# Memory stage of a decoder kernel: gated values formed on GpSimd in token layout

## The reference

```
sim = einsum('pbnhd,hkpd->bn..', q, keys)              # 8 heads, 2 sides, 32 keys
s, i = top_k(sim, 8) on both sides; scores = top 8 of the 64 sums
o = einsum('bnd,bnhkd->bnhk', inputs, key_in[idx])     # inputs . down vector
o = gelu(o, approximate=False) * softmax(scores)
return einsum('bnhk,bnhkd->bnd', o, key_out[idx])
```

## Time and profile before

| what | value |
|---|---|
| median of three runs | 2621.1 us |
| profiled execution, its own time | 2621.93 us |
| its span, first to last instruction | 2620.1 us |
| mean granted TensorE clock | 0.951 of full speed |
| PE busy | 2343.8 us (89%) |
| PEld busy | 1855.1 us (71%) |
| DVE busy | 2078.6 us (79%) |
| ACT busy | 1887.8 us (72%) |
| POOL busy | 836.3 us (32%) |
| memory stage, L1243's first start to the end of L1846's last | 583.7 us to 1309 us |

### The profile page before, as it was taken

The page is one execution under the profiler, slowest core; times in us unless marked ns, Lnnn a source line. Parts: engine busy times, 40 slices in busy tenths (PEclk is TensorE's granted clock), DMA queues, the critical chain, the costliest instruction groups (busy, mean ns, idle before and its releaser), DMA issues.

```text
span 2620.1 us, 95472 instructions
## 1 busy us (share of the span) xinstructions
PE 2343.8 (89%) x34892; PEld 1855.1 (71%) x34892; DVE 2078.6 (79%) x5455; ACT 1887.8 (72%) x3592; POOL 836.3 (32%) x1203
## 2 busy tenths in 40 slices
PE   2999943966999999999889999899899999999999
PEld 1676632645888888888857667566688788888887
DVE  6788889668899999999667777688766777777776
ACT  1888852777688888878467777788567777777776
POOL 1455510336566666666333333233100000000000
PEclk9999975987899999999899999899799999999999
DMA  5000000000000000000020000111011111111111
GB/s 183 1 0 0 0 17 1 1 0 3 2 0 0 0 0 0 0 0 0 3 66 0 0 0 0 36 43 44 30 43 46 49 56 52 57 51 54 52 57 45
DMA packets 56808, 64.82 MB, mean 25 GB/s; under 512 B 7696, under 2 KB 35088, under 8 KB 56592
## 3 DMA queue, kind: packets, MB, share of 16 engines
q1 hardware_dynamic: 56720, 63.65, 7.9%
HBM read 59.17 MB, written 4.46 MB: 24 GB/s over the span
## 4 chain that ended last, share of the span: by engine, by line
PE 68%; DVE 17%; issue 9%; ACT 2%; SPq 1%; DVEq 1%; POOL 1%; ACTq 0%; POOLq 0%; DMA 0%
PE ps L1075 5%; PE ps L1118 5%; PE ps L1103 5%; PE ps L1348 4%; PE ps L1370 4%; PE ps L1372 4%; PE ps L1371 4%; PE ps L1350 4%; PE ps L1349 4%; PE ps L1131 3%; PE ps L1090 3%; DVE work L1829 2%; PE ps L1248 2%; DVE work L1830 2%; DVE work L1836 2%
## 5 line engine op out<-in xcount | busy, mean ns | idle before, releaser
L559 POOL TENSOR_TENSOR work<-work,consts_sb 128x1024 f32<-128x1024 f32 x128 | 245.9, 1921 | 387.8 <-ACT work L727 346.9
L1260 PE MATMUL ps<-work 32*32 32x32 f32 x16384 | 249.5, 224 | 45.7 <-DVE work L1779 31.6
L1260 PEld LDWEIGHTS ps<-work 32*32 32x32 f32 x16384 | 242.2, 145 | 60.3 <-issue 60.3
L1988 DVE TENSOR_TENSOR h_low<-consts_sb,h_up 128x1024 fp32r<-128x1024 f32 x128 | 156.7, 1224 | 116.1 <-ACT h_up L964 116.1
L1586 DVE TENSOR_REDUCE work<-ps 128x8 f32<-128x512 f32 x256 | 169.8, 686 | 86.0 <-PE ps L1075 80.1
L1348 PE MATMUL ps<-a_low,w_up 128*128 128x512 f32 x512 | 205.9, 402 | 0.0
L1370 PE MATMUL ps<-h_low,d_up 128*128 128x512 f32 x512 | 199.9, 390 | 2.3 <-DVE h_low L1988 2.3
L1350 PE MATMUL ps<-a_up,w_low 128*128 128x512 f32 x512 | 200.7, 392 | 0.0
L1349 PE MATMUL ps<-a_up,w_up 128*128 128x512 f32 x512 | 200.6, 392 | 0.0
L1372 PE MATMUL ps<-h_up,d_low 128*128 128x512 f32 x512 | 199.5, 390 | 0.0
L1371 PE MATMUL ps<-h_up,d_up 128*128 128x512 f32 x512 | 199.2, 389 | 0.0
(11 more groups left out here) (297 smaller groups left out, 6271.5 us busy)
## 6 DMA issues: line engine op xcount, KB each, us to landing
gates_spread<-gate_rows SPq DMA_DIRECT2D x128, 256.0 KB, 3.1
ctxT_all<-in_ctxT SPq DMA_DIRECT2D x1, 4096.0 KB, 12.9
work<-in_ctx SPq DMA_DIRECT2D x64, 64.0 KB, 1.7
work<-in_ctxT SPq DMA_DIRECT2D x64, 64.0 KB, 1.7
out<-x_all SPq DMA_DIRECT2D x16, 256.0 KB, 3.5
big<-in_up SPq DMA_DIRECT2D x1, 2048.0 KB, 8.5
consts_sb<-in_consts SPq DMA_DIRECT2D x1, 936.0 KB
w<-in_key_inT SPq DMA_DIRECT2D x1, 512.0 KB, 3.3
```

Source lines behind the costliest of these rows:

```text
L559: pool.tensor_tensor(KX[:, u].rearrange("p b (h k) -> p b h k", h=PER_SET), KC[:, u].unsqueeze(2).to_broadcast([P, 2, PER_SET, SEQ]), own_ ...
L1260: ins = pe.matmul(psW[rows, n // 16, :, n % 16], XT[rows, T.u, :, n], YT[rows, T.u, :, n], start=True, stop=True)
L1988: dve.tensor_tensor(h_low[:, n], hid[n], h_up[:, n].bitcast(F32), ALU.subtract).then_inc(h_split, 1)
```

## The change

The gating moves from the expert layout to the token layout. `hidden` on TensorE now has the tile's tokens as the stationary operand (two matmuls of 512 columns), so gelu's output lies with tokens on partitions. Because the stationary operand is taken from a fixed buffer, SyncE copies each tile of xT into XH (a transfer from SBUF to SBUF) two tiles ahead. GpSimd's new segment `gated` multiplies WT with HT in place, TensorE's `turn_gated` transposes the product into psG, and ScalarE's new segment `copy_gated` copies psG to HG. VectorE's `gated` is gone. The lags behind it grow by one: `turn_gated` 6, `mixed` 7, `add_memory` 6, the statistics 8. IN2 becomes two buffers, and `terms` waits for `scaled_one_hots` of two tiles earlier.

```diff
--- before.py
+++ after.py
@@ -250,15 +250,16 @@
         Z = carve(2 * PH).rearrange("p (u h) -> p u h", u=2)
         FLOOR = carve(2 * PH).rearrange("p (u h) -> p u h", u=2)
         RZ = carve(2 * PH).rearrange("p (u h) -> p u h", u=2)
-        hots = carve(3 * 2 * NS).rearrange("p (r s h k) -> p s r h k", r=3, s=2, h=PH)
-        IN2 = hots[:, :, 2]
+        hots = carve(4 * 2 * NS).rearrange("p (r s h k) -> p s r h k", r=4, s=2, h=PH)
+        IN2 = [hots[:, :, 2 + u] for u in range(2)]
         KI = carve(NEXP)
         sides = carve(8 * NS)
         XY = sides.rearrange("p (k n h) -> p n h k", n=8, h=PH)
         XT = carve(2 * NEXP).rearrange("p (u k t) -> p u k t", u=2, k=NKEY)
         YT = carve(2 * NEXP).rearrange("p (u k t) -> p u k t", u=2, k=NKEY)
         WT = carve(NEXP)
-        HT = carve(2 * NEXP).rearrange("p (u c d) -> p u c d", u=2, c=CHUNKS)
+        HT = carve(2 * NEXP).rearrange("p (u n) -> p u n", u=2)
+        XH = carve(2 * P).rearrange("p (u d) -> p u d", u=2)
         HG = w8[:, 0:NEXP].rearrange("p (c d) -> p c d", c=CHUNKS)
 
 
@@ -285,7 +286,7 @@
         x_side, y_side = [sides.rearrange("p (k a n) -> p k a n", k=NKEY, a=4)[:, :, a:4:2] for a in range(2)]
 
         def one_hots_of(u):
-            return hots[:, :, u:3:2 - u]
+            return hots[:, :, u:4:2]
 
         HC = HID // P
         QUAD = 4
@@ -363,7 +364,7 @@
         psW = ps[:, 0:2, :].rearrange("p q (k t) -> p q k t", k=NKEY)
         psABOVE = ps[:, 2:4, :].rearrange("p q (n h k) -> p (q n) h k", n=2, h=PH)
         psG = ps[:, 4:6, :].rearrange("p b (c d) -> p (b c) d", d=P)
-        psH = ps[:, 6:8, :].rearrange("p b (c d) -> p (b c) d", d=P)
+        psH = ps[:, 6:8, :]
         psM = bank(4, 0)
         psSim = ps[:, 0, :]
 
@@ -430,8 +431,9 @@
         scaled_ready, best_less_ready = sem("scaled_one_hots_ready"), sem("best_less_ready")
         share_ready, xy_ready, sides_ready, spread_done, back_ready, back_turned = (
             sem("share_ready"), sem("xy_ready"), sem("sides_ready"), sem("spread_done"), sem("back_ready"), sem("back_turned"))
-        h_done, h_ready, hg_ready, m_done = sem("h_done"), sem("h_ready"), sem("hg_ready"), sem("m_done")
+        h_done, h_ready, gated_ready, hg_ready, m_done = sem("h_done"), sem("h_ready"), sem("gated_ready"), sem("hg_ready"), sem("m_done")
         y_used_x, y_used_m = sem("xout_used"), sem("memory_used")
+        raw_in = [sem("raw_tile0_in"), sem("raw_tile1_in")]
 
         lg_done, lg_ready, lg_less_max, le_ready = sem("lg_done"), sem("lg_ready"), sem("lg_less_max"), sem("le_ready")
         a_step, a_split, w_step, w_split = sem("a_step"), sem("a_split"), sem("w_step"), sem("w_split")
@@ -484,6 +486,12 @@
                 sp.dma_start(kout[NKEY * j:NKEY * j + NKEY], key_out.rearrange("(a c j) d -> j a c d", a=NKEY, c=CHUNKS)[j])\
                     .then_inc(tables, 16)
 
+            sp.wait_ge(phase, PHASE["memory"])
+
+            def raw_tile(T):
+                need(sp, h_done, T.before(2))
+                sp.dma_start(XH[:, T.u, :], xTt[:, T.t, :]).then_inc(raw_in[T.u], 16)
+            staggered(nc, sp, NT, [(0, raw_tile)])
             sp.wait_ge(phase, PHASE["attn1"])
             sp.dma_start(up_w, up.rearrange("e p h -> p e h")).then_inc(experts_in, 16)
             sp.dma_start(down_w, down.rearrange("e (c p) d -> p e c d", p=P)).then_inc(experts_in, 16)
@@ -623,16 +631,15 @@
                 x, y = keys_of(u)[:, 0], keys_of(u)[:, 1]
                 second = best_of(u)[:, :, :, 1:2].to_broadcast([P, 2, PH, NKEY])
                 rest, deep, wide = [terms_of(u)[:, n] for n in (REST, DEEP_X, WIDE_Y)]
-                need(pool, hot_ready, T.before(1))
-                need(pool, scaled_ready, T.before(1))
-                pool.tensor_tensor(IN2, keys_of(u), second, ALU.subtract).then_inc(less_second, 1)
+                need(pool, scaled_ready, T.before(2))
+                pool.tensor_tensor(IN2[u], keys_of(u), second, ALU.subtract).then_inc(less_second, 1)
                 pool.tensor_tensor(wide, y, second[:, 0], ALU.mult)
                 pool.wait_ge(less_second, T.now())
                 pool.sem_inc(rank_seen, 1)
-                pool.tensor_scalar(IN2, IN2, 0.0, None, ALU.is_ge).then_inc(in2_ready, 1)
+                pool.tensor_scalar(IN2[u], IN2[u], 0.0, None, ALU.is_ge).then_inc(in2_ready, 1)
                 pool.wait_ge(in2_ready, T.now())
                 pool.sem_inc(rank_seen, 1)
-                pool.tensor_scalar(rest, IN2[:, 0], -1.0, 1.0, ALU.mult, ALU.add).then_inc(far_ready, 1)
+                pool.tensor_scalar(rest, IN2[u][:, 0], -1.0, 1.0, ALU.mult, ALU.add).then_inc(far_ready, 1)
                 pool.wait_ge(far_ready, T.now())
                 pool.tensor_tensor(rest, rest, x, ALU.mult).then_inc(rest_ready, 1)
                 pool.wait_ge(rest_ready, T.now())
@@ -641,9 +648,16 @@
             def second_one_hot(T):
                 pool.wait_ge(far_ready, T.now())
                 pool.wait_ge(top_ready, T.now())
-                pool.tensor_tensor(IN2, IN2, hots[:, :, T.u], ALU.subtract).then_inc(hot_ready, 1)
-
-            staggered(nc, pool, NT, [(0, candidates), (1, second_one_hot), (0, terms)])
+                pool.tensor_tensor(IN2[T.u], IN2[T.u], hots[:, :, T.u], ALU.subtract).then_inc(hot_ready, 1)
+
+            def gated(T):
+
+                u = T.u
+                pool.wait_ge(h_ready, T.now())
+                pool.wait_ge(back_ready, T.now())
+                pool.tensor_tensor(HT[:, u], WT, HT[:, u], ALU.mult).then_inc(gated_ready, 1)
+
+            staggered(nc, pool, NT, [(0, candidates), (3, gated), (1, second_one_hot), (0, terms)])
 
             pool.wait_ge(phase, PHASE["attn1"])
             staggered(nc, pool, NT, [(0, spread(ATTN["attn1"]))])
@@ -895,10 +909,15 @@
                 ins.then_inc(share_ready, 1)
 
             def hidden(T):
-                need(act, hg_ready, T.before(2))
+                need(act, back_turned, T.before(2))
                 act.wait_ge(h_done, T.now())
-                act.activation(HT[:, T.u], psH, ACT.Gelu).then_inc(h_ready, 1)
-            staggered(nc, act, NT, [(0, normed), (2, exps_before_gelu), (5, hidden), (2, exps_after_gelu), (2, best_one_hot), (3, above_floor),
+                act.activation(HT[:, T.u].rearrange("p (b n) -> p b n", b=2), psH, ACT.Gelu).then_inc(h_ready, 1)
+
+            def copy_gated(T):
+                act.wait_ge(back_turned, T.now())
+                need(act, m_done, T.before(1))
+                act.activation(HG, psG, ACT.Copy).then_inc(hg_ready, 1)
+            staggered(nc, act, NT, [(0, normed), (2, exps_before_gelu), (5, hidden), (2, exps_after_gelu), (2, best_one_hot), (6, copy_gated), (3, above_floor),
                                     (3, scaled_one_hots)])
 
 
@@ -1244,8 +1263,9 @@
 
             def hidden(T):
                 need(pe, h_ready, T.before(1))
-                for c in range(CHUNKS):
-                    ins = pe.matmul(psH[:, c, :], KI[:, c * P:c * P + P], xTt[:, T.t, :], start=True, stop=True)
+                pe.wait_ge(raw_in[T.u], T.pair * 16 + 16)
+                for b in range(2):
+                    ins = pe.matmul(psH[:, b, :], XH[:, T.u, :], KI[:, b * WIDE:b * WIDE + WIDE], start=True, stop=True)
                 ins.then_inc(h_done, 1)
 
             def spread_heads(T):
@@ -1260,12 +1280,12 @@
                         ins = pe.matmul(psW[rows, n // 16, :, n % 16], XT[rows, T.u, :, n], YT[rows, T.u, :, n], start=True, stop=True)
                 ins.then_inc(spread_done, 1)
 
-            def turn_weights(T):
-                pe.wait_ge(back_ready, T.now())
+            def turn_gated(T):
+                pe.wait_ge(gated_ready, T.now())
                 need(pe, hg_ready, T.before(1))
                 need(pe, y_used_m, T.before(1))
                 for c in range(CHUNKS):
-                    ins = pe.transpose(psG[:, c, :], WT[:, c * P:c * P + P], ident)
+                    ins = pe.transpose(psG[:, c, :], HT[:, T.u, c * P:c * P + P], ident)
                 ins.then_inc(back_turned, 1)
 
             def mixed(T):
@@ -1273,7 +1293,7 @@
                 for c in range(CHUNKS):
                     ins = pe.matmul(psM, HG[:, c, :], kout[:, c, :], start=c == 0, stop=c == CHUNKS - 1)
                 ins.then_inc(m_done, 1)
-            staggered(nc, pe, NT, [(6, mixed), (0, key_scores), (4, hidden), (5, turn_weights), (4, spread_heads)])
+            staggered(nc, pe, NT, [(7, mixed), (0, key_scores), (6, turn_gated), (4, hidden), (4, spread_heads)])
 
 
             b1 = ATTN["attn1"]
@@ -1832,14 +1852,8 @@
             def turn_back(T):
 
                 dve.wait_ge(spread_done, T.now())
-                need(dve, back_turned, T.before(1))
+                need(dve, gated_ready, T.before(1))
                 dve.transpose(WT, psW.rearrange("p q k t -> p k q t")).then_inc(back_ready, 1)
-
-            def gated(T):
-                dve.wait_ge(h_ready, T.now())
```

(7 more changed lines are left out.)

## The result

| | kernel before | changed kernel |
|---|---|---|
| median on the same chip | 2622.09 us | 2726.39 us (2725.09 to 2731.24, 4 runs) |
| ratio | | 1.0404, 95% interval 1.0385 to 1.0423 |
| span of the profiled execution | 2620.1 us | 2725.6 us |

The change costs 104 us. The forecast was slower by 58 us, 2680 us with a range of 2655 to 2710. The direction is right, the time lies outside the range.

A forecast was written before the change was run, and what follows sets the result against it. VectorE was taken to bound the memory stage at 10.56 us a step; a loop of 11.55 us replaces it. Eight slow tiles and 52 steps give +56.4, with drain +58: 2680 us on 2621.9, range 2655 to 2710.

The forecast's parts named there:

- What VectorE loses, and what bounds before: Memory stage: VectorE's list bounds at 10.56 us a step; L1842 goes, 1.27 us a tile, leaving about 9.3 us.
- ScalarE's loop: From key_scores through transposes, copy, above_floor, scaled one-hots, turn_sides and turn_back to the next key_scores: 11.55 us a step.
- The two hand-overs: Estimated at 0.06 us each, transposes to ScalarE and scaled one-hots to VectorE; at most a step of 11.7 to 11.9.
- Beside the loop: Spread ends about 8.0 us after key_scores, turn_back starts at 10.2, mixed ends about then: they have room.
- VectorE 1.6 us slack: VectorE idles 1.6 us a step awaiting ScalarE's input for chosen; GpSimd can delay it only within this room.
- faster rival: Copy doesn't hold ScalarE; TensorE's loop through spread and mixed rules at 10.34 us: 2616, at best 2605 us; chance 5%.
- The rival with the clock: TensorE's pause ahead of key_scores lowers its clock: +0.94 us a step, 2734 us, or 2698 in a third; chance 10%.
- The rival with GpSimd: GpSimd's product takes 2.54 us or more, excluding VectorE's L1788: 0.3 us in 52 steps, +15, 2695 us; chance 10%.
- VectorE at some 83%: Sign expected in the profile after: VectorE's busy share in the middle of the memory stage, with steps of 11.5 us.
- The slow steps at the start: Written-out first tiles of the memory stage: eight slow tiles instead of six, 13.1 us each.
- The drain: One more step drains at the end of the memory stage: 2 us, between 0 and 5.
- Behind the stage: Time after the memory stage: the forecast had 0 us more.

The follow-up runs named there:

- split4: Changed kernel with GpSimd's 1024-column product cut into four instructions of 256 columns; 2693.09 us, ratio 1.0256.
- fill: Changed kernel with hidden's two matmuls issued twice with the same result in every step; 2709.35 us, ratio 1.0341.
- fill_first: Changed kernel with hidden issued twice only in the written-out steps, not inside the loop; 2740.95 us, ratio 1.0455.
- fill_odd: Changed kernel with hidden issued twice in every second tile; 2716.95 us, ratio 1.0368.
- copylast: Changed kernel with ScalarE's copy of psG moved to the end of ScalarE's list; 2714.84 us, ratio 1.0335.
- tuned: Changed kernel, product in four pieces behind terms, transposes behind hidden, ScalarE's copy last, add_memory one lag later behind top_keys; 2615.80 us, ratio 0.9976.
- fill_split4: Changed kernel with hidden issued twice and GpSimd's product in four pieces; 2713.21 us, ratio 1.0344.
- before_moved: Kernel before with unread semaphore increments on TensorE, ScalarE and GpSimd ahead of cross1; 2621.50 us, ratio 0.9997.
- before_two_in2: Kernel before with only the second IN2 buffer and the looser wait of terms, gating still on VectorE; 2646.45 us, ratio 1.0101.
- tuned_two: Changed kernel with all lists reordered as in tuned, GpSimd's product in two pieces of 512 columns; 2614.66 us, ratio 0.9970.
- split4_copylast: Changed kernel with GpSimd's product in four pieces and ScalarE's copy at the end of its list; 2682.32 us, ratio 1.0207.
- tuned_whole: Changed kernel with all lists reordered as in tuned, GpSimd's product left as one instruction; 2651.72 us, ratio 1.0111.

## Why the prediction was wrong in its size

- **What VectorE loses, and what bounds before:** right. L1842 is gone, VectorE is no longer full.
- **ScalarE's loop, 11.55 us:** right as a loop, and not what ruled. L1288 starts 0.86 to 0.96 us after L1262 and the copy waits for it in each of 64 steps (192.1 us in all). In split4 and fill, where L1808 isn't held by the product, it rules, with steps of 11.60 and 11.59 us. The two hand-overs that I estimated are within that.
- **"Beside the loop: the spread and `mixed` of the same step have room", and VectorE 1.6 us slack:** this step failed. It worked out both at durations of the kernel before, L1808 at 0.45 us and `mixed` at 2.05. They take 1.39 us (median) and up to 3.17. L1824, which the forecast didn't name, takes 0.57 us for 0.15. So the loop through `less_best`, spread, `mixed` and `add_memory`, which the forecast had at 10.34 us in its faster rival, rose to 12.23 us. 52 x (12.23 - 11.55) = 35 us, the whole miss of the middle.
- **The rival with the clock (10%)** had the pause ahead of `key_scores` and the loss in `key_scores`. Here the pause stands ahead of the spread and the loss in `mixed` (L1262 takes 1.02 to 1.13 us). Where the pause does stand ahead of `key_scores`, in split4, the clock is 0.99. Its "in a third of the steps, 2698" has the right kind of size for the wrong instruction.
- **The rival with GpSimd (10%)** had the instruction right. I put the product at 1.90 us from the earlier trace rows; it takes 2.36, nearer to the 2.54 that is twice L644. The other error is that I counted its exclusion against a fixed slack. The Trainium skill, "SBUF — State Buffer", section "SBUF: two separate sides", has such a pair exclude each other for a whole instruction. By that rule I allowed 12.1 us at most. The trace agrees with the rule: L1808 ends 0.15 us behind L658, and in fill, where it comes at the same moment, GpSimd gives way. What I missed was not the rule but that a held L1808 makes the next one late, so that the hold lasts; in fill_first a late `mixed` started it.
- I gave each of the two rivals a chance of its own, as if they were independent. In split4 and fill they go together: fill has a clock of 1.00 and L1808 at 0.24 us, split4 0.99 and 0.37, after 0.89 and 1.39. They are not one thing either, as the later part of fill_odd shows.
- **VectorE at some 83%** as a sign: my own terms give (10.56 - 1.27) / 11.55 = 80%. Measured were 90%, in part because the time in which L1808 and L1824 are held counts as busy: 1.55 and 0.57 us a step on average, for 0.57 and 0.15 before.
- **The slow steps at the start:** 14.05 us each, not 13.1, +7.6 us. In split4 they take 13.59, in copylast 13.72, in tuned 13.34, which suggests that the product and the copy each have a part in it; the rest was not separated.
- **The drain:** 1.1 us for 2.
- **Behind the stage** I had nothing; 5.85 us came, 5.5 of them in cross1. The cause is open.

The sum with these sizes: +12.4 + 86.6 + 1.1 + 5.85 - 0.5 = +105.5 us, to rounding.

In short: the step that failed is that the spread and `mixed` had room beside ScalarE's loop. With L1808 held, L1824 held and `mixed` late, their own loop was the longest, 12.23 us against 11.55.

## What to carry to other kernels

When work moves to another engine, don't take the durations of small instructions beside it from the trace of before: ask which of them can fall on a long GpSimd instruction and what a delay there makes late, and cut the long one or order the lists so that they don't meet. A held VectorE instruction can make the same instruction late in the next step, and a late TensorE group can start that. Here cutting the product, or filling every step's pause, each brought the step down by 0.63 us, some 33 us in 52 steps, and both together brought no more; filling every second step didn't end the hold. A long wait of an engine off the path can be useful: letting GpSimd start `terms` earlier, with no work changed, cost 24 us.

## What was new about the hardware

- A VectorE instruction with a single SBUF operand waits for GpSimd as well: L1824, fp32, 128x8, takes 0.15 us alone and 0.57 us beside L636 (0.63 us), and 1.01 us as the median in fill_split4, beside L651 (1.27 us). It ends 0.03 us behind them. In fill L1808, recorded 0.05 us after the start of L658, passed in 0.23 us, and L658 took 2.51 us there in place of 2.36: here it was GpSimd that gave way.
- GpSimd's fp32 product of 128x1024 takes 2.36 us with two full operands; L559, same size, takes 1.90 us, and 256 columns take 0.73.
- 1.7 us of doubled matmuls per step raised the granted clock from 0.89 to 1.00 and shortened the step by 0.64 us.
- What a fall of the clock costs hangs on what runs then: the spread of 32x32 matmuls takes 3.86 us at a granted clock of 0.57 and 3.85 at 1.00 (fill_odd, 1105 and 1117 us), `mixed` 3.08 in place of 2.05.
- The cross1 stage, of the same code everywhere, takes 196.9 to 197.4 us in before, before_moved and before_two_in2 and 202.7 to 203.1 in after, fill, fill_first, tuned and tuned_two, all at a granted clock of 0.95. Each is of one profiled execution. The weight loads of L1145 (L1164 after) wait longer: 33.4 us in 65 times before, 42.0 in 65 after. What sets this difference was not found. Beyond it the time goes with the clock of the stage: 205.1 us at 0.94 in fill_odd, about 207.5 at 0.92 in split4, copylast, split4_copylast and tuned_whole, and 212.1 at 0.90 in fill_split4. Why the clock differs there was not found either.
